# Gating VectorE's long operations on the scatters of a four-layer graph network

## What is computed

```python
h = jnp.maximum(_layernorm(x, axis=-1), 0.0)
x = x + _L0_gnn_ref(h, edge_index, edge_attr_3, ...)   # Gaussian mixture of 6 kernels, mean over edges
x = x + _L1_gnn_ref(h, edge_index, ...)                # two SAGE convolutions, 32 -> 64 -> 32
x = x + _L2_gnn_ref(h, edge_index, edge_attr_3, ...)   # spline convolutions with 5**3 kernels
x = x + _L3_gnn_ref(h, edge_index, ...)                # two SAGE convolutions, 32 -> 64 -> 32
# in _L0: msg = einsum('eko,ek->eo', xg[src], gauss); agg = segment_sum(msg, dst)
# in _L2: msg = einsum('es,eso->eo', basis, gathered); out = segment_sum(msg, row)
```

## Time and profile before

| | before |
|---|---|
| median of three runs | 10463.64 us |
| the profiled execution | 10493.68 us, its span 10491.6 |
| GpSimd (POOL) busy | 6325.7 us, 60% |
| VectorE (DVE) busy | 6368.4 us, 61% |
| TensorE (PE) busy, mean granted clock | 6169.3 us, 59%, 0.678 |
| scatters in A, C, D | 832 of 998 ns, 880 of 991, 944 of 1024 |
| scatters in S, four passes | 544 of 1162 ns |
| scatters to the new cells, of messages | 944 of 974 ns, 1792 of 981 |

### The profile page before, as it was taken

The page is one execution under the profiler, slowest core; times in us unless marked ns, Lnnn a source line. Parts: engine busy times, 40 slices in busy tenths (PEclk is TensorE's granted clock), DMA queues, the critical chain, the costliest instruction groups (busy, mean ns, idle before and its releaser), DMA issues. The chain is left out here.

```text
span 10491.6 us, 187901 instructions
## 1 busy us (share of the span) xinstructions
PE 6169.3 (59%) x48488; PEld 5174.2 (49%) x48489; DVE 6368.4 (61%) x19749; ACT 2334.7 (22%) x6546; POOL 6325.7 (60%) x6534
## 2 busy tenths in 40 slices
PE   5444056665777766666456576655554555546575
PEld 5443045554777754444445555334444444445454
DVE  8996086664666659999547665731111544458565
ACT  0000034443333322222104040011111222204040
POOL 3777637776777767777434146257776777724151
PEclk9999988887555558888567575655555555557575
DMA  6990012222433322222395566680000111136565
GB/s 210 302 201 7 26 44 86 85 85 76 115 104 106 104 71 62 65 66 66 65 231 209 125 224 158 134 100 17 14 14 11 35 34 34 34 74 239 111 224 113
DMA packets 1315188, 1070.73 MB, mean 102 GB/s; under 512 B 894004, under 2 KB 1157417, under 8 KB 1306047
## 3 DMA queue, kind: packets, MB, share of 16 engines
q1 hardware_dynamic: 954526, 693.52, 25.9%
q0 software_dynamic: 225216, 300.54, 8.7%
q10 hardware_dynamic: 135264, 74.60, 3.1%
HBM read 518.16 MB, written 591.91 MB: 106 GB/s over the span
## 5 line engine op out<-in xcount | busy, mean ns | idle before, releaser
L2822 POOL DMA_INDIRECT msg<-row,idx x1792 | 1758.1, 981 | 608.5 <-issue 524.8
L1179 POOL DMA_INDIRECT run_rows<-rec,idx x544 | 632.1, 1162 | 1320.2 <-ACT rec L1157 1174.3
L2581 POOL DMA_INDIRECT cell<-rec,idx x944 | 919.9, 974 | 504.6 <-issue 284.3
L2392 POOL DMA_INDIRECT cell<-rec,idx x944 | 966.8, 1024 | 334.0 <-issue 286.8
L2047 POOL DMA_INDIRECT rec_d<-rec,idx x880 | 872.5, 991 | 454.0 <-issue 267.0
L516 POOL DMA_INDIRECT rec_r<-sc_rec,sc_idx x832 | 830.1, 998 | 431.0 <-issue 283.5
L2803 PE MATMUL ps<-w_stn,hft 128*128 x1792 | 609.6, 500 | 365.2 <-ACT hft L2731 341.5
L837 DVE TENSOR_TENSOR oh<-iota_f,rd 128x128 f32<-128x128 f32 x948 | 217.8, 289 | 951.4 <-PE ps L2503 950.6
L1137 PE MATMUL ps<-planes,hot 128*128 x8704 | 568.0, 224 | 334.4 <-DVE hot L1119 172.0
L2518 PE MATMUL ps<-h_rows,oht 128*128 x1888 | 450.9, 403 | 525.2 <-ACT oht L2525 524.9
L1119 DVE TENSOR_SCALAR hot<-loc,lane_c 128x512 bf16<-128x512 bf16 x2176 | 662.7, 382 | 123.9 <-PE ps L1137 66.1
(11 more groups left out here) (448 smaller groups left out, 15754.3 us busy)
## 6 DMA issues: line engine op xcount, KB each, us to landing
loc<-loc_s SPq DMA_DIRECT2D x68, 2048.0 KB
got<-run_rows SPq DMA_DIRECT2D x472, 224.0 KB
got<-rec_d SPq DMA_DIRECT2D x236, 416.0 KB
rec_d<-padd SPq DMA_DIRECT2D x4, 12480.0 KB
rec_d<-padd SPq DMA_DIRECT2D x4, 12064.0 KB
msg<-zpad SPq DMA_DIRECT2D x8, 5390.0 KB
got<-msg SPq DMA_DIRECT2D x220, 196.0 KB
cin<-cell SPq DMA_DIRECT2D x224, 136.0 KB, 2.2
```

The lines of the kernel that those rows point to most:

```text
L1179: nc.gpsimd.indirect_dma_start(out=out, out_offset=bass.IndirectOffsetOnAxis(ap=idx[:, u, m % HU:m % HU + 1], axis=0), in_=rec[:, m, :], i ...
L2392: nc.gpsimd.indirect_dma_start(out=cells, out_offset=bass.IndirectOffsetOnAxis(ap=idx[:, n, g:g + 1], axis=0), in_=rec[:, n, g, :], in_off ...
L2581: nc.gpsimd.indirect_dma_start(out=cells, out_offset=bass.IndirectOffsetOnAxis(ap=idx[:, n, g:g + 1], axis=0), in_=rec[:, n, g, :], in_off ...
L2822: nc.gpsimd.indirect_dma_start(out=msgs, out_offset=bass.IndirectOffsetOnAxis(ap=idx[:, m, g:g + 1], axis=0), in_=row[:, m, g, :], in_offs ...
```

## The change

- A new semaphore `begun` in each of the four passes. GpSimd first adds a credit to it, and then 1 behind every scatter. VectorE waits for it before its long operations: in A before the one-hots (3k + 1, credit 24) and before the product with them (3k + 5), in C before the one-hots (4k + 1, credit 32) and before `basis` (4k + 2), in D before the one-hots (4k + 1, credit 28) and before the product (4(k + 3) + 2), in S before each set (k + 1, credit 5).
- These operations are made in one piece instead of four: 512 elements in A, 512 and 500 in C, 512 and 768 in D; in S two of 1024 instead of four of 512. `spread` and `weigh` come whole too, without a gate.
- In A the product with the one-hots moves ahead of the small sum onto `upto` (L439), and LATE goes from 18 to 21.
- `hots_by_tile` goes; `pick_hot` makes the same four pieces itself.

```diff
-            for B in s["parts"]:
-                made = nc.vector.tensor_tensor(s["hot"][:, m, :, B, :], bcast(iota_f[:, 0:CELLS].unsqueeze(1).unsqueeze(1), shape),
-                                               bcast(key[:, :, B].unsqueeze(3), shape), ALU.is_equal)
-            made.then_inc(s["s_hot"], 1)
+            v.wait_ge(begun, count)
+            nc.vector.tensor_tensor(s["hot"][:, m, :, :, :], bcast(iota_f[:, 0:CELLS].unsqueeze(1).unsqueeze(1), shape),
+                                    bcast(key.unsqueeze(3), shape), ALU.is_equal).then_inc(s["s_hot"], 1)
...
             v.wait_ge(s["s_with"], k + 1)
+            v.wait_ge(begun, count)
+            nc.vector.tensor_tensor(sel, sel, s["hot"][:, m, :, :, :], ALU.mult).then_inc(s["s_sel"], 1)
             nc.vector.tensor_tensor(upto, upto, at[:, :, G, :], ALU.add).then_inc(s["s_next"], 1)
-            for B in s["parts"]:
-                taken = nc.vector.tensor_tensor(sel[:, :, B, :], sel[:, :, B, :], s["hot"][:, m, :, B, :], ALU.mult)
-            taken.then_inc(s["s_sel"], 1)
...
+        AHEAD_OF_SCATTERS = 3 * 2 * GN // G
...
+            nc.gpsimd.sem_inc(s["begun"], AHEAD_OF_SCATTERS)
...
                             bounds_check=last_row, oob_is_err=False).then_inc(s["sent"][n], 16)
+                        nc.gpsimd.sem_inc(s["begun"], 1)
...
-            NG, LATE = EJ // STEP, 18
+            NG, LATE = EJ // STEP, 21
...
-                        rank_hot(v, ranks, keys[:, :, ds(j, G)], k, m)
+                        rank_hot(v, ranks, keys[:, :, ds(j, G)], k, m, rings["begun"], 3 * k + 1)
...
+            LAG = 5
...
                                 v.wait_ge(s_pick, k + 1)
+                                v.wait_ge(s_begun, k + 1)
                                 for w in range(SUPER):
-                                    for e in (slice(0, HR * P), slice(HR * P, RUN * P)):
-                                        made = nc.vector.tensor_scalar(hot[:, m % RING, w, e], loc[:, u, m % HU, e], lane_c[:, w:w + 1], None,
-                                                                       ALU.is_equal)
+                                    made = nc.vector.tensor_scalar(hot[:, m % RING, w, :], loc[:, u, m % HU, :], lane_c[:, w:w + 1], None,
+                                                                   ALU.is_equal)
...
+            LAG = 5 + AHEAD
...
+                        nc.gpsimd.sem_inc(s_begun, G * LAG)
...
-                            hots_by_tile(oh[:, m % RING, :, :], rrt[:, u, T, RLOC]).then_inc(s_hot, 1)
+                            v.wait_ge(s_begun, G * k + 1)
+                            hot_of(oh[:, m % RING, :, :], rrt[:, u, T, RLOC]).then_inc(s_hot, 1)
...
+                            v.wait_ge(s_begun, G * k + 2)
+                            nc.vector.tensor_tensor(basis[:, m % RING, :, 0:KW].rearrange("p g (a b) -> p g a b", b=KS),
+                                                    bcast(pair[:, m % 2, :, :].unsqueeze(3), [P, G, KS * KS, KS]),
+                                                    bcast(h[:, :, 2, :].unsqueeze(2), [P, G, KS * KS, KS]), ALU.mult).then_inc(s_basis, 1)
...
+            LAG = 4
...
-                            hots_by_tile(oh[:, n % RING, :, :], got[:, n, :, XW + MLOC]).then_inc(s_hot, 1)
+                            v.wait_ge(s_begun, G * k + 1)
+                            hot_of(oh[:, n % RING, :, :], got[:, n, :, XW + MLOC]).then_inc(s_hot, 1)
...
+                            v.wait_ge(s_begun, G * (k + AHEAD) + 2)
+                            nc.vector.tensor_tensor(prod[:, n % 2, :, :].rearrange("p g (k o) -> p g k o", k=KG), picked,
+                                                    bcast(by.unsqueeze(3), [P, G, KG, C]), ALU.mult).then_inc(s_prod, 1)
...
+                        nc.gpsimd.sem_inc(s_begun, G * (LAG + AHEAD))
```

More of the change, by code:

```diff
@@ L413, in rank_rings @@
             J = upto.shape[1]
-            s = dict(bank=bank, upto=upto, J=J, parts=[slice(g, g + 2 // J) for g in range(0, G, 2 // J)])
+            s = dict(bank=bank, upto=upto, J=J)
             s["hot"], s["sel"] = sb_in(c, "bin_hot", [P, R, J, G, CELLS], BF16), sb_in(c, "bin_sel", [P, 2, J, G, CELLS])
@@ L493, in build @@
         NTURN = EJ // (2 * GN)
+        AHEAD_OF_SCATTERS = 3 * 2 * GN // G
         def scatter_rings(c, words):
             return dict(idx=sb_in(c, "sc_idx", [EP, 2, GN], I32), rec=sb_in(c, "sc_rec", [EP, 2, GN, words]),
-                        fed=sem_in(c, "fed"), sent=[sem_in(c, f"sent{n}") for n in range(2)])
+                        fed=sem_in(c, "fed"), begun=sem_in(c, "begun"), sent=[sem_in(c, f"sent{n}") for n in range(2)])
         def scatter_feed(act, s, placed, row, rec, i, first):
@@ L832, in hot_of @@
                                            bcast(local.unsqueeze(2), [P, G, P]), ALU.is_equal)
-        def hots_by_tile(oh, local):
-            for g in range(G):
-                made = nc.vector.tensor_tensor(oh[:, g, :], iota_f[:, :], bcast(local[:, g:g + 1], [P, P]), ALU.is_equal)
-            return made
         def one_hot(oh, rec, t, word):
@@ L1087, in send_runs @@
                 sent = [sem_in(c, f"sent{u}") for u in range(2)]
-                s_hot, s_pick, s_fill, s_idx = (sem_in(c, n) for n in ("hot", "picked", "filled", "indexed"))
+                s_hot, s_pick, s_fill, s_idx, s_begun = (sem_in(c, n) for n in ("hot", "picked", "filled", "indexed", "begun"))
                 def all_sets(eng, turn):
@@ L1919, in source_order_pass @@
                 (s_k, s_diff, s_sq, s_scaled, s_ex, s_meta, s_ramp, s_hat, s_hot, s_cast, s_turned, s_copied, s_pick, s_pair, s_basis,
-                 s_sum, s_add, s_fill, s_const, s_away) = (sem_in(c, n) for n in (
+                 s_sum, s_add, s_fill, s_const, s_away, s_begun) = (sem_in(c, n) for n in (
                      "chain", "diff", "square", "scaled", "exponent", "meta", "ramps", "hats", "hot", "cast", "turned", "copied", "picked", "pair",
-                     "basis", "summed", "added", "filled", "consts", "away"))
+                     "basis", "summed", "added", "filled", "consts", "away", "begun"))
                 room = oh[:, :, :, :].rearrange("p r g w -> p (r g w)")
@@ L2218, in destination_order_pass @@
                 turned = [ps[:, q, 0:P * G // 2].bitcast(BF16) for q in (4, 7)]
-                s_w, s_one, s_hot, s_cast, s_turned, s_copied, s_pick, s_prod, s_m0, s_fill = (sem_in(c, n) for n in (
-                    "weights", "ones", "hot", "cast", "turned", "copied", "picked", "product", "message", "filled"))
+                s_w, s_one, s_hot, s_cast, s_turned, s_copied, s_pick, s_prod, s_m0, s_fill, s_begun = (sem_in(c, n) for n in (
+                    "weights", "ones", "hot", "cast", "turned", "copied", "picked", "product", "message", "filled", "begun"))
                 s_got = [sem_in(c, f"got{n}") for n in range(UBD)]
@@ L2528, in pick_hot @@
             v.wait_ge(s["turned"], k + 1)
-            hots_by_tile(s["oh"][:, n, :, :], rd[:, ds(t, G), LOC]).then_inc(s["hot"], 1)
+            for g in range(G):
+                made = nc.vector.tensor_tensor(s["oh"][:, n, g, :], iota_f[:, :], bcast(rd[:, ds(t + g, 1), LOC], [P, P]), ALU.is_equal)
+            made.then_inc(s["hot"], 1)
         def to_cells(nodes, pitch, F, cells, load_weights, blank):
```

38 lines of the change are left out of this document (14 added, 24 removed).

## The result

The changed kernel takes 10602.7 us, the median of four runs (10599.5 to 10606.4), beside 10462.7 us of the kernel before: 1.0133 times as long, 95% interval 1.0115 to 1.0151. The forecast was 10743. Its direction was right; of +279 us, +140 came.

The account below looks back on a forecast made before the run. GpSimd's back-to-back scatters bound the four passes; A +104, C +137, D +88, S -50 sum to +279 on the profiled 10491.6 us, 10743 us after 30 off for the median; own range 10600 to 10850, 8 in 10: 10365 to 10860.

Parts of the forecast that it names:

- The law of 0.13 us: All passes: a VectorE operation with two SBUF inputs, running when a scatter is 0.13 us old, holds it until its end.
- Where the gate opens: Gated passes: with 12 scatters queued, gates open at a scatter's end; operations start 0.24 us before the next, costing 0.32 us.
- Rival 2: A, C, D: released operations start past a scatter's reads, so lengthenings vanish; about -95 us, 10369 us; chance 0.25.
- C, +137: Source-order pass: 220 x (0.32 + 0.31) us, plus 0.06 for the pair, less 15, makes +137 us.
- A, +104: Natural-order pass: 168 gated batches cost 108 us, 40 unbound ones 16, less today's 20, makes +104 us.
- the gate binds from batch 35 to 40, for some 168 of 208: Natural-order pass: VectorE drifts ahead 0.6 scatters a batch until its gate holds it, in 168 batches at 0.64 us.
- D, +88: Destination-order pass: gates don't bind; 236 batches x 0.57 us, less 47, makes +88 us (bounds -7 and +165).
- hot and product make a stretch of 1.55 us, longer than the period: Destination-order pass: one-hots and product run without a gap, so each batch covers at least one scatter's point, costing 0.57 us.
- S, -50: Pass `send_runs`: fewer operations leave gaps, long scatters go, about 50 of 102 us return (bounds -100 and +60).
- Increments, zero: POOL's sequencer: 3200 added `begun` increments cost nothing, at most 0.08 us each, 256 us.
- Rival 1: All four passes: nothing waits at its gate, merged operations keep today's phases; 10613 us; chance 0.15.

Follow-up runs that it names:

- the filler: Changed kernel plus a sum over 448 constant columns between gate and operation: in C 10462.3 us; in D, with LAG 2 in place of 4, 10531.1 us.
- the lead of 15: Changed kernel with pass A's credit at 15 scatters in place of 24: 10583.8 us, ratio 1.0126; 12247 us on a slower chip.

## Why the prediction was right and wrong

- **The law of 0.13 us** held for whole operations: in A, C and D of after 877 scatters are longer by over 0.1 us or should be, and 837 of them agree with it to 0.04 us. Most of the others met an operation that began just before the point and held nothing. In C the filler showed that the phase decides. For rows of short pieces the law is not enough, as D of the kernel before shows. Right for what the change makes.
- **Where the gate opens** (queue of 12, at a scatter's end, 0.24 us before the next start): right, on the earlier trace rows. Rival 2, that it spares the scatters, needed a start about 0.45 us later; the filler made a start 0.53 us later, and the scatters went to 995 and 978 ns.
- **C, +137**: measured +125, with 0.35 and 0.32 us for each held operation and 193 of 220 held. Right.
- **A, +104**: measured +27. The failed step is "the gate binds from batch 35 to 40, for some 168 of 208": seven of 416 gates held. The step took a batch 0.4 us shorter than the 3.65 of before. It left out that the sum onto `upto` moves behind the product, which stands in the change's own diff: TensorE waits for that sum, VectorE for TensorE, and the batch was 3.73. It also let the drift run on through GpSimd's pauses, where each one opens the gates by 11 us again. With the old order the pass is 94 us longer than before the change, with 110 of 208 held.
- **D, +88**: measured +18. That D's gates open early was right (in 213 of 236 batches the one-hots begin when 4k-35 scatters have begun, and the gate opened at 4k-39). The failed step is "hot and product make a stretch of 1.55 us, longer than the period". The one-hots alone held one scatter, and the product behind them none. 0.57 us per batch was 0.28, 236 x 0.28 = 65 us of longer scatters. The kernel before could have told it: its pieces of one-hots and product, in the rows of 3054 to 3056 a stretch of 2 us without a gap, cost only 47 us in the whole of D.
- **S, -50**: -30 (16 to 37), -48 on the profiled executions. That the long scatters go was right; that the mean falls near 1.0 was not, it stayed at 1.10. The size came from one execution, 30 us slower than the median. GpSimd doesn't issue back to back in S, as the working says of all four passes: it sat idle for 1320 us.
- **Increments, zero**: right; the pause between scatters is 0.30 us as before.
- Rival 1 has the nearest time, 10613, by another road: C's gates did bind, and A and D cost less than it says.
- The direction came from C: what A and D added, S took away. A and D together were forecast at +192 and gave +45. The range of 10600 to 10850 isn't the sum of its bounds either: with D's and S's upper ones it would reach 10930.
- The Trainium skill (SBUF — State Buffer, Who interferes with whom) says that a VectorE operation with two SBUF inputs contends with GpSimd's reads; C's held operations agree, by 0.35 and 0.32 us each. Its inference that a tensor_tensor doesn't stall descriptor generation is contradicted by C's 1134 ns against 995 with the same operations at another phase.

## What to carry to other kernels

Here an increment that GpSimd's sequencer raised behind a scatter came at the end of a scatter, twelve before it, and so just ahead of the next one's start. To slip an operation between two starts, it helped to wait for the increment and then for 0.53 us more of harmless work; other delays weren't tried. Whether a gate binds is a race of two periods: any reordering in the same change that alters one of them must be in the sum, and so must the pauses that set the race back. And a stretch of back-to-back operations needn't act as one operation: look how long such a stretch already is before the change, and what it costs.

## What the chip showed beyond that

- A scatter that is held by one VectorE operation goes on at its end even when the next has already begun (D above), so pieces protect in most cases even without pauses; in D of the kernel before 27 scatters were held over such borders all the same, by 12 of the 47 us.
- Behind four memsets of one element the next operation begins 0.01 us after the first of them; they don't delay it.
- At a pause of GpSimd its sequencer stood for 14 to 22 us and then raised its increments 0.57 us apart, so that one gate held VectorE for long and those of the next ten batches and more did not.
- A's gates, of which only seven held, went with another step of VectorE and GpSimd, for 24 us of longer scatters (A with and without gates).
- The same kernel takes 10450 us on some chips and 12450 to 12630 on others, where GpSimd waits longer for records (in A 626 us with the lead of 15, and 147 on the first kind). Why they differ isn't shown. D lost time there with the shorter lead that cost it nothing on the first kind.
